# TensorE's order rewritten so that matmuls of one array mode stand together, PSUM's banks as they were

## The chip, the cores and the metric

The kernel runs on one core of a Trainium2 chip. The metric is the device time of the whole program in microseconds, the median of several runs. The five engines (TensorE or PE, VectorE or DVE, ScalarE or ACT, Pool, and SyncE which issues the DMAs) each run their own instruction list in order and meet only through semaphores.

## The reference

Eight blocks ("batches") of 512 tokens by 256 features go through one adaptive-layer-norm transformer block:

```python
h = _layernorm(x, axis=-1) * (1 + ca) + sa
x = x + ga * _L0_attn_ref(h, ...)      # 16 heads of 16 features, softmax over 512 keys
h = _layernorm(x, axis=-1) * (1 + cb) + sb
x = x + gb * _L0_ffn_ref(h, ...)       # 2 shared and 16 routed experts (top 4), gelu
```

All 18 experts are computed for all tokens: up (256 to 128 features), gelu, times the gate (zero for experts not chosen), down (128 to 256). ca, sa, ga, cb, sb, gb come from one small product per batch.

## The kernel before

**Staging.** A software pipeline runs over batches. One iteration i does attention for batch i, the projections for batch i + 1, and the experts of batches i - 1 and i - 2 (`true_item` gives each kind its lag). An iteration has four sets, s = 0 to 3; a set is one group of four heads. `slot_order(s)` (line 70) writes a set's order by hand as a list of items (kind, number); every engine walks the same list and does its part of each item it knows. So this list is TensorE's order, and VectorE's, ScalarE's and Pool's too. `NO_MAX` (line 67) and `EXTRAS` place items by slot.

**A set.** A set has U = 16 slots, then the ups, then pv:

- in a slot, `max` (one score matmul of the next head group; VectorE reduces it to a row maximum, `neg_max`, line 765) and `exp` (one transposed score matmul of this group; ScalarE takes its exponent into `probs`, line 573). Both have 64 rows of contraction. Units of even number use array rows 0 to 63, odd ones 64 to 127 (`unit`, at = 64 * (u % 2)). Moving size 512. TensorE's line is 871.
- between them 20 or 16 `down` items a set (three full-array matmuls each, line 960; accumulated in two `down_bank`s), and the extras: transposes of the attention output (`oT`, line 913), of normalised rows (`onT`, `h1T`, `h2T`, line 905), products `wo`, `qk`, `v`, `logit` (line 822), the gates' transpose `gateT` (944), VectorE's norms (`stats`, `rows`, lines 629 to 639), the router's top four (`top`, lines 690 to 701) and `final`.
- then four or five `up` items (six full-array matmuls each, line 822; ScalarE gelu, line 618, VectorE times the gate, line 755, ScalarE and Pool split into two half-precision parts, lines 563 and 529), `maxT` (the transposed maxima, line 878, copied by VectorE into the score operand, line 773, which the next set's `exp` matmuls wait for), and `pv` (four items of four 32-column matmuls in float32, line 894, into `pv_bank`, which VectorE copies to `o_raw` at the end of the set, line 812).
- the first two `exp` of the next set (EARLY = 2) stand in the pv part.

Before, a slot issues one max and one exp. A few slots have no max (`NO_MAX`), so two or three maxima of a set are left over for the ups.

**Banks.** PSUM's eight banks: two `vector_bank`s, used in turn by every item of `V_KINDS` (max, maxT, oT, wo, v, logit, gateT), three `scalar_bank`s in turn for `R_KINDS` (exp, onT, h1T, qk, h2T, up), one `pv_bank`, two `down_bank`s. `ring` gives each item its bank by its place in the order; `wait_bank` makes TensorE wait until the bank's user before has been read. No bank of either kind can be filled while its previous content is unread, and TensorE's list goes on only after the wait.

Of the kernel before, what the change touches and what calls it, by code (L numbers as in the profile page):

```python
# [57 lines left out]
EARLY = 2  # L58
# [5 lines left out]

NO_MAX = {0: (3, 5, 8), 1: (0, 11, 12), 2: (0, 10), 3: (0, 15)}


def slot_order(s):  # L70


    out = []
    maxima = [("max", (s + 1) * U + u) if s < 3 else ("max0", u) for u in range(U)]
    downs = [("down", d) for d in range(TT * SETS[DOWN_SET[s]], TT * SETS[DOWN_SET[s] + 1])]
    ups = [("up", c) for c in range(*SETS[UP_SET[s]:UP_SET[s] + 2])]
    for u in range(U):
        out += EXTRAS.get((s, u), [])
        if u not in NO_MAX[s]:
            out.append(maxima.pop(0))  # L80
        if u >= EARLY:
            out.append(("exp", s * U + u))
        left = U - 1 - u
        while downs and len(downs) * (U - 1) > left * TT * SETLEN:
            out.append(downs.pop(0))
    assert not downs
    for j, up in enumerate(ups):
        out += EXTRAS.get((s, U + j), [])
        if j == 3:
            out += maxima + [("maxT", s + 1) if s < 3 else ("maxT0", 0)]  # L90
            maxima = []
        out.append(up)
        if j < 2:
            out += maxima[:2]
            maxima = maxima[2:]
        if j >= 1:
            out.append(("gated", up[1] - 1))
        if j >= 3:
            out.append(("pv", s * TT + j - 3))
    out.append(("gated", ups[-1][1]))  # L100
    for kc in range(len(ups) - 3, TT):
        out.append(("pv", s * TT + kc))
        if kc >= TT - EARLY:
            out.append(("exp", (s + 1) * U + kc - TT + EARLY) if s < 3 else ("exp0", kc - TT + EARLY))
    return out


# [9 lines left out]
def true_item(item):  # L117

    kind, n = item
    if kind in ("max0", "maxT0", "exp0"):  # L120
        return kind[:-1], n, 1
    if kind in ("h1T", "qk", "v", "stats1", "rows1"):
        return kind, n, 1
    if kind == "up" or kind == "gated":
        return kind, n, -1 if SET_OF[n] < 2 else -2
    if kind == "down":
        return kind, n, -1 if SET_OF[n // TT] < 1 else -2
    if kind == "final":
        return kind, n, -2
    return kind, n, 0 if kind in ("max", "maxT", "exp", "pv", "xg") else -1  # L130


def ring(kinds, banks):
# [31 lines left out]
def block_kernel(nc, x, c_t, wmod, wqkvo, bqk_in, bv, bo, w_up, w_down, router, out):  # L165
# [7 lines left out]
    with ctx:  # L173
# [449 lines left out]
        def _(dve):  # L623
# [92 lines left out]
            def body(i, par):  # L716
                nb, pb = i + 1, i - 1
                x_post, z = x_post2[1 - par], z2[1 - par]
                for s in range(G):
                    for item, kind, n, b in items(i, s):  # L720
# [27 lines left out]
                        if kind == "gated" and n >= NSH:  # L748

                            g = gelu[:, n % NGELU, :]  # L750
                            wait(dve, taken["up"], NEX, b, n + 1)
                            quarter, rest = divmod(n - NSH, 4)
                            if rest == 0:
                                wait(dve, s_gld[quarter % 2], 32, b, 16 * (quarter // 2 + 1))
                            dve.tensor_tensor(g, g, gates[:, (n - NSH) % 8, :], ALU.mult).then_inc(s_gated, 1)  # L755
                        if item[0] not in V_KINDS:
                            continue
                        src = bank(item)
# [46 lines left out]
                        elif kind == "gateT":  # L805
                            wait(dve, s_gst, 16, b, 0)
                            dve.tensor_copy(gate_rows, src[0:NR, :]).then_inc(done, 1)

                    if exists(i):
                        wait(dve, made["pv"], G * TT, i, TT * (s + 1))  # L810
                        wait(dve, made["oT"], 4, i, 0)
                        dve.tensor_copy(o_raw[:, s, :], OB[:]).then_inc(taken["pv"], 1)

            iterations(dve, body)

# [179 lines left out]
```

## Time and profile before

| | |
|---|---|
| median of 3 runs | 1061.0 us (1059.8 to 1061.09) |
| the profiled execution | 1056.59 us, span 1054.8 us |
| PE busy | 942.0 us (89%), 5928 matmuls |
| DVE busy | 677.4 us (64%) |
| ACT busy | 630.0 us (60%) |
| POOL busy | 379.3 us (36%) |
| mean granted TensorE clock | 0.945 |
| maxima (line 765) | 512, mean 688 ns |
| exponents (line 573) | 512, mean 603 ns |

The profile is of one execution. Busy time of PE is modelled with overlapping matmuls, so the start of one matmul to the start of the next says more than its duration. In a timeline row the columns are start, duration, engine, line, operation, output and inputs, tile and shapes, count, and in brackets the idle time before it and who ended it. "PEclk" is the granted share of full clock.

### The profile page before, as it was taken

What the parts mean: (1) busy time and instruction counts of PE and PEld (TensorE: products, weight loads), DVE (VectorE), ACT (ScalarE), POOL (GpSimd) and SP (SyncE); (2) the same over time, 40 slices, a digit from 0 to 9 for tenths busy, and PEclk for the clock granted to TensorE, in tenths of its full rate; (3) what the DMA queues carried; (4) which work ended last, traced back from release to release, by engine and by line L of the source; (5) the groups of instructions that cost most, each with busy time, mean ns of one, the idle gap of its engine ahead of it and who ended that gap; (6) DMA issues with size and microseconds to landing.
All of it is one profiled execution on the core that took longest, in us unless ns stands there. A gap on an engine that the chain in (4) does not pass through costs nothing.

```text
span 1054.8 us, 17394 instructions
## 1 busy us (share of the span) xinstructions
PE 942.0 (89%) x5928; PEld 423.0 (40%) x5928; DVE 677.4 (64%) x1315; ACT 630.0 (60%) x1033; POOL 379.3 (36%) x325
## 2 busy tenths in 40 slices
PE   5468786889999999999999999999999999997897
PEld 3112222324444354434444354444444453345564
DVE  5665767656776777676866567676866677724333
ACT  3145644556676758666775647666675757662343
POOL 4331222232442434243433324243434332344354
PEclk9658978989999999999999989999999999999899
DMA  6811600352016210342017210352016200311220
GB/s 217 170 45 36 111 1 1 68 144 101 1 36 141 96 61 4 86 144 101 1 36 180 86 36 1 87 146 101 1 36 177 77 24 1 107 65 40 74 113 21
DMA packets 50428, 78.53 MB, mean 74 GB/s; under 512 B 8216, under 2 KB 44568, under 8 KB 46240
## 3 DMA queue, kind: packets, MB, share of 16 engines
q1 hardware_dynamic: 50336, 77.36, 26.2%
q8 instruction: 51, 0.84, 0.4%
q14 instruction: 41, 0.34, 0.1%
HBM read 64.31 MB, written 12.89 MB: 73 GB/s over the span
## 4 chain that ended last, share of the span: by engine, by line
PE 73%; DVE 9%; DMA 4%; ACT 4%; issue 4%; POOL 2%; SPq 2%; DVEq 0%; POOLq 0%; ACTq 0%
PE scalar_bank L822 20%; PE down_bank L960 19%; PE vector_bank L871 11%; PE pv_bank L894 10%; DVE neg_max L765 5%; PE scalar_bank L871 5%; PE vector_bank L822 4%; PE scalar_bank L905 2%; PE vector_bank L913 2%; ACT probs L573 1%; SPq L389 1%; DMA gates_by_expert<-rows 1%; DMA k_parts<-qk_lo 1%; POOL act_lo L529 1%; DMA gates<-gates_by_expert 1%
## 5 line engine op out<-in xcount | busy, mean ns | idle before, releaser
L765 DVE TENSOR_REDUCE neg_max<-vector_bank 128x1 f16<-128x512 f32 x512 | 339.4, 688 | 143.2 <-PE vector_bank L871 133.2
L573 ACT ACTIVATE probs<-scalar_bank 128x512 f32<-128x512 f32 x512 | 290.6, 603 | 206.4 <-PE scalar_bank L871 203.6
L529 POOL TENSOR_TENSOR act_lo<-gelu,act_hi 128x512 f16<-128x512 f32 x144 | 177.3, 1251 | 201.9 <-ACT act_hi L563 192.0
L871 PE MATMUL vector_bank<-k_aug,q_aug 64*128 64x512 f16 x512 | 194.6, 413 | 42.7 <-DVE neg_max L765 25.7
L871 PE MATMUL scalar_bank<-q_aug,k_aug 64*128 64x512 f16 x512 | 200.0, 406 | 9.7 <-ACT f_ring L546 3.3
L960 PE MATMUL down_bank<-down_hi,act_hi 128*128 128x256 f16 x576 | 163.3, 283 | 0.3
L960 PE MATMUL down_bank<-down_lo,act_hi 128*128 128x256 f16 x576 | 159.9, 278 | 0.0
L960 PE MATMUL down_bank<-down_hi,act_lo 128*128 128x256 f16 x576 | 159.6, 277 | 0.0
L755 DVE TENSOR_TENSOR gelu<-gelu,gates 128x512 f32<-128x512 f32 x128 | 110.6, 885 | 69.6 <-ACT gelu L618 59.5
L618 ACT ACTIVATE gelu<-scalar_bank 128x512 f32<-128x512 f32 x144 | 85.1, 596 | 76.4 <-PE scalar_bank L822 54.7
L894 PE MATMUL pv_bank<-probs,v_aug 128*32 128x512 f32 x1024 | 130.6, 620 | 0.0
L563 ACT ACTIVATE act_hi<-gelu 128x512 f16<-128x512 f32 x128 | 79.9, 627 | 50.2 <-DVE gelu L755 50.1
L822 PE MATMUL scalar_bank<-z_hi,up_hi 128*128 128x512 f16 x288 | 109.8, 381 | 0.0
L822 PE MATMUL scalar_bank<-z_lo,up_hi 128*128 128x512 f16 x288 | 109.2, 379 | 0.0
L822 PE MATMUL scalar_bank<-z_hi,up_lo 128*128 128x512 f16 x288 | 109.2, 379 | 0.0
L871 PEld LDWEIGHTS vector_bank<-k_aug,q_aug 64*128 64x128 f16 x512 | 43.2, 94 | 160.2 <-issue 79.8
L960 PEld LDWEIGHTS down_bank<-down_hi,act_hi 128*128 128x128 f16 x576 | 56.4, 98 | 96.3 <-issue 87.4
L477 POOL TENSOR_TENSOR z_lo<-f_ring,z_hi 128x512 f16<-128x512 f32 x32 | 37.2, 1174 | 128.4 <-ACT f_ring L602 86.7
L871 PEld LDWEIGHTS scalar_bank<-q_aug,k_aug 64*128 64x128 f16 x512 | 45.8, 94 | 87.6 <-issue 58.0
L477 POOL TENSOR_TENSOR qk_lo<-f_ring,qk_hi 128x512 f16<-128x512 f32 x32 | 37.0, 1156 | 105.1 <-ACT f_ring L594 104.6
L773 DVE COPY q_aug<-vector_bank 1x512 f16<-1x512 f16 x128 | 53.9, 421 | 11.9 <-PE vector_bank L878 10.2
L960 PEld LDWEIGHTS down_bank<-down_hi,act_lo 128*128 128x128 f16 x576 | 57.4, 100 | 7.7
(122 smaller groups left out, 1104.8 us busy)
## 6 DMA issues: line engine op xcount, KB each, us to landing
gates<-gates_by_expert SPq DMA_DIRECT2D x32, 1024.0 KB, 4.7
q_aug<-q_parts SPq DMA_DIRECT2D x48, 128.0 KB, 3.9
k_aug<-k_parts SPq DMA_DIRECT2D x48, 128.0 KB, 4.5
x_pre<-in_x SPq DMA_DIRECT2D x8, 512.0 KB, 6.0
x_post<-in_x SPq DMA_DIRECT2D x8, 512.0 KB, 3.9
out<-x_post SPq DMA_DIRECT2D x8, 512.0 KB, 5.0
gates<-in_w_up SPq DMA_DIRECT2D x4, 576.0 KB, 11.6
gates<-in_w_down SPq DMA_DIRECT2D x4, 576.0 KB, 5.5
```

The source lines that it names most:

```text
L477: pool.tensor_tensor(lo, f_ring[:, n % 2, :], hi, ALU.subtract).then_inc(s_lo, 1)
L529: pool.tensor_tensor(act[1][:, c, :], gelu[:, n % NGELU, :], act[0][:, c, :], ALU.subtract).then_inc(s_elo, 1)
L563: scalar.activation(act[0][:, c, :], gelu[:, n % NGELU, :], ACT.Copy).then_inc(s_ehi, 1)
L573: scalar.activation(probs[:, n % U, :], src[:], ACT.Exp, scale=SCALE).then_inc(taken[kind], 1)
L618: scalar.activation(gelu[:, n % NGELU, :], src[:], ACT.Gelu).then_inc(taken[kind], 1)
L755: dve.tensor_tensor(g, g, gates[:, (n - NSH) % 8, :], ALU.mult).then_inc(s_gated, 1)
L765: dve.tensor_reduce(neg_max[:, (u // 2) % TT, at:at + 1], src[:], AX.X, ALU.max, negate=True).then_inc(done, 1)
L773: ins = dve.tensor_copy(qa[at:at + 1, 2 * n + j // 2, :], src[:].bitcast(F16)[32 * j:32 * j + 1, 0:S])
L822: ins = pe.matmul(dst, a, b, start=n == 0, stop=n == len(terms) - 1)
L871: pe.matmul(dst[:], st[at:at + 64, pair, t * P:(t + 1) * P], mo[at:at + 64, pair, :], start=True, stop=True).then_inc(sig, 1)
L894: ins = pe.matmul(o, v_aug[par][:, kc, at], probs[:, u, :], start=kc == 0, stop=kc == TT - 1)
L960: ins = pe.matmul(o, act[a][:, c - SETS[SET_OF[c]], t * P:(t + 1) * P], wd[w][:, c, :], start=c == 0 and k == 0 and t % 2 == 0, stop=c == ...
```

## The change

`slot_order` is rewritten, and with it the order of all engines. Two slots become one: two maxima, then two exponents, then the downs of two slots. No slot is without a maximum, `NO_MAX` is gone, and none are left for the ups. `maxT` stands two ups after the slots, not three. The two early exponents stand before pv, together, and the four pv items follow one another. VectorE's copy of `pv_bank` to `o_raw` becomes an item of its own, `oraw`, at the end of the set. The banks' number and the rule of turns stay; which item has which bank follows from the new order.

```diff
--- before.py
+++ after.py
@@ -64,44 +64,34 @@
 
 
 
-NO_MAX = {0: (3, 5, 8), 1: (0, 11, 12), 2: (0, 10), 3: (0, 15)}
-
-
 def slot_order(s):
 
 
     out = []
     maxima = [("max", (s + 1) * U + u) if s < 3 else ("max0", u) for u in range(U)]
+    early = [("exp", (s + 1) * U + u) if s < 3 else ("exp0", u) for u in range(EARLY)]
     downs = [("down", d) for d in range(TT * SETS[DOWN_SET[s]], TT * SETS[DOWN_SET[s] + 1])]
     ups = [("up", c) for c in range(*SETS[UP_SET[s]:UP_SET[s] + 2])]
     for u in range(U):
         out += EXTRAS.get((s, u), [])
-        if u not in NO_MAX[s]:
-            out.append(maxima.pop(0))
-        if u >= EARLY:
-            out.append(("exp", s * U + u))
+        if u % 2:
+            out += maxima[u - 1:u + 1]
+            out += [("exp", s * U + v) for v in (u - 1, u) if v >= EARLY]
         left = U - 1 - u
         while downs and len(downs) * (U - 1) > left * TT * SETLEN:
             out.append(downs.pop(0))
     assert not downs
     for j, up in enumerate(ups):
         out += EXTRAS.get((s, U + j), [])
-        if j == 3:
-            out += maxima + [("maxT", s + 1) if s < 3 else ("maxT0", 0)]
-            maxima = []
+        if j == 2:
+            out.append(("maxT", s + 1) if s < 3 else ("maxT0", 0))
         out.append(up)
-        if j < 2:
-            out += maxima[:2]
-            maxima = maxima[2:]
         if j >= 1:
             out.append(("gated", up[1] - 1))
-        if j >= 3:
-            out.append(("pv", s * TT + j - 3))
+    out += early
     out.append(("gated", ups[-1][1]))
-    for kc in range(len(ups) - 3, TT):
-        out.append(("pv", s * TT + kc))
-        if kc >= TT - EARLY:
-            out.append(("exp", (s + 1) * U + kc - TT + EARLY) if s < 3 else ("exp0", kc - TT + EARLY))
+    out += [("pv", s * TT + kc) for kc in range(TT)]
+    out.append(("oraw", s))
     return out
 
 
@@ -127,7 +117,7 @@
         return kind, n, -1 if SET_OF[n // TT] < 1 else -2
     if kind == "final":
         return kind, n, -2
-    return kind, n, 0 if kind in ("max", "maxT", "exp", "pv", "xg") else -1
+    return kind, n, 0 if kind in ("max", "maxT", "exp", "pv", "oraw", "xg") else -1
 
 
 def ring(kinds, banks):
@@ -753,6 +743,11 @@
                             if rest == 0:
                                 wait(dve, s_gld[quarter % 2], 32, b, 16 * (quarter // 2 + 1))
                             dve.tensor_tensor(g, g, gates[:, (n - NSH) % 8, :], ALU.mult).then_inc(s_gated, 1)
+                        if kind == "oraw":
+
+                            wait(dve, made["pv"], G * TT, b, TT * (n + 1))
+                            wait(dve, made["oT"], 4, b, 0)
+                            dve.tensor_copy(o_raw[:, n, :], OB[:]).then_inc(taken["pv"], 1)
                         if item[0] not in V_KINDS:
                             continue
                         src = bank(item)
@@ -805,11 +800,6 @@
                         elif kind == "gateT":
                             wait(dve, s_gst, 16, b, 0)
                             dve.tensor_copy(gate_rows, src[0:NR, :]).then_inc(done, 1)
-
-                    if exists(i):
-                        wait(dve, made["pv"], G * TT, i, TT * (s + 1))
-                        wait(dve, made["oT"], 4, i, 0)
-                        dve.tensor_copy(o_raw[:, s, :], OB[:]).then_inc(taken["pv"], 1)
 
             iterations(dve, body)
```

The order of a set's TensorE items, as both functions give it, for set 3 before (cut) and after (cut):

```
before: max0 | down0 down1 | max1 exp50 | down2 | max2 exp51 | down3 | max3 exp52 | down4 down5 | ... up5 | max14 max15 | up6 up7 maxT up8 | pv12 | up9 | pv13 pv14 | exp0 | pv15 | exp1
after:  max0 max1 | down0 1 2 | max2 max3 exp50 exp51 | down3 4 5 | max4 max5 exp52 exp53 | down6 7 | ... up5 up6 maxT up7 up8 up9 | exp0 exp1 | pv12 13 14 15
```

## Rows read from the trace of the kernel before

**Rows 1.** The page's chain of work that ended last: shares of the span by engine.

```profile
PE 73%; DVE 9%; DMA 4%; ACT 4%; issue 4%; POOL 2%; SPq 2%; DVEq 0%; POOLq 0%; ACTq 0%
```

**Rows 2.** Windows, one steady iteration: stretch, length, busy time of each engine, granted clock.

```profile
479.30:595.60 116.30, 112.23 (x738) 49.90 (x737) 82.39 (x162) 79.02 (x130) 43.15 (x38) 1.00 0.27 76
```

**Rows 3.** Waits of PE over the whole run: total us, times, longest.

```profile
PE vector_bank L871 <- DVE neg_max L765: 25.7, 51, 1.9
```

**Rows 4.** Timeline of PE, a slot of set 3 with one down.

```profile
582.79 0.39 PE L871 MATMUL vector_bank<-k_aug,q_aug 64*128 64x512 f16 x1
582.79 0.39 PE L871 MATMUL scalar_bank<-q_aug,k_aug 64*128 64x512 f16 x1
583.11 0.28 PE L960 MATMUL down_bank<-down_hi,act_hi 128*128 128x256 f16 x1
...
583.34 0.27 PE L960 MATMUL down_bank<-down_hi,act_lo 128*128 128x256 f16 x1
583.54 0.39 PE L871 MATMUL vector_bank<-k_aug,q_aug 64*128 64x512 f16 x1
```

**Rows 5.** Timeline of PE, start of set 0.

```profile
486.47 0.60 PE L871 MATMUL vector_bank<-k_aug,q_aug 64*128 64x512 f16 x2
487.00 0.28 PE L960 MATMUL down_bank<-down_hi,act_hi 128*128 128x256 f16 x1
```

**Rows 6.** Timeline, two maxima in different banks, and VectorE's start on the first.

```profile
592.63 0.39 PE L871 MATMUL vector_bank<-k_aug,q_aug 64*128 64x512 f16 x2
...
592.95 0.39 PE L822 MATMUL scalar_bank<-z_hi,up_hi 128*128 128x512 f16 x1
...
593.05 0.70 DVE L765 TENSOR_REDUCE neg_max<-vector_bank 128x1 f16<-128x512 f32 x1 [2.11 <-PE vector_bank L871]
```

**Rows 7.** Timeline, wo's last matmul, its reading, and two maxima queued behind.

```profile
500.62 0.27 PE L822 MATMUL vector_bank<-wqkvo_hi,z_lo 128*128 128x256 f16 x1
...
500.93 0.69 DVE L790 TENSOR_TENSOR rows<-vector_bank,ga_all 128x512 f32<-128x512 f32 x1 [0.98 <-PE vector_bank L822]
...
501.54 1.28 DVE L765 TENSOR_REDUCE neg_max<-vector_bank 128x1 f16<-128x512 f32 x2
```

**Rows 8.** Timeline of PE: first up and last pv of the sets 0 to 3.

```profile
506.25 0.38 PE L822 MATMUL scalar_bank<-z_hi,up_hi 128*128 128x512 f16 x1
...
515.63 1.06 PE L894 MATMUL pv_bank<-probs,v_aug 128*32 128x512 f32 x8
...
536.52 0.39 PE L822 MATMUL scalar_bank<-z_hi,up_hi 128*128 128x512 f16 x1
...
545.91 1.06 PE L894 MATMUL pv_bank<-probs,v_aug 128*32 128x512 f32 x8
...
566.07 0.38 PE L822 MATMUL scalar_bank<-z_hi,up_hi 128*128 128x512 f16 x1
...
576.57 1.06 PE L894 MATMUL pv_bank<-probs,v_aug 128*32 128x512 f32 x8
...
591.24 0.38 PE L822 MATMUL scalar_bank<-z_hi,up_hi 128*128 128x512 f16 x1
```

**Rows 9.** Timeline of ACT, second reader of a transposed bank.

```profile
495.63 0.59 ACT L602 ACTIVATE f_ring<-scalar_bank 128x512 f32<-128x512 f32 x1
```

**Rows 10.** Timeline of DVE in set 1: norm's rows, router's first step, next maximum.

```profile
521.38 2.96 DVE L639 TENSOR_SCALAR rows<-x_pre,mean_var,rstd 128x256 f32<-128x256 f32 x4
...
529.87 0.40 DVE L690 MAX8 top<-logits 128x8 f32<-128x16 f32 x4
...
532.32 0.68 DVE L765 TENSOR_REDUCE neg_max<-vector_bank 128x1 f16<-128x512 f32 x1
```

**Rows 11.** Timeline of an early iteration without ups: pv and the copies of the maxima.

```profile
138.03 3.96 PE L894 MATMUL pv_bank<-probs,v_aug 128*32 128x512 f32 x24
138.14 1.72 DVE L773 COPY q_aug<-vector_bank 1x512 f16<-1x512 f16 x4 [0.77 <-PE vector_bank L878]
```

**Rows 12.** Windows, a stretch of the first iteration.

```profile
50.00:80.00 30.00, 20.33 (x72) 4.11 (x71) 20.97 (x41) 11.39 (x19) 8.32 (x5) 0.52 0.13 40
```

## The prediction

> **What bounds the kernel now.** I read the chain of work first: 73% of the span is TensorE, no other engine has more than 9% [rows 1]. Then one steady iteration by windows: TensorE is busy 112.2 of 116.3 us at full clock, VectorE 82, ScalarE 79 [rows 2]. Then the waits: TensorE stood 25.7 us in the whole run for VectorE's maxima [rows 3]. So it is TensorE's order, back to back, and what it costs is read in the timeline of PE [rows 4]: a maximum (64 rows, lower or upper half) and an exponent score (other half) start in the same hundredth, 582.79; the next full-array matmul starts 0.32 us later, at 583.11; the three "down" matmuls follow at 0.11 to 0.12 us, and after the last (583.34) the next score starts 0.20 us later. Two matmuls of one half follow at 0.21 us (two take 0.60, one 0.39) [rows 5]. So a score stream is 0.22, and each edge between array modes costs 0.10: a trip into the score mode and back is 0.22 + 2 x 0.10, about 0.41 us.
>
> The Trainium skill, "TensorEngine Tiling (Array Packing)", section "Key Properties", says that changing the tiling mode drains TensorE; by that rule, the trace agrees, with 0.10 us an edge.
>
> **What is removed on TensorE.** I counted the stretches of one mode in the order that both versions of `slot_order` give, set by set: 38, 36, 35, 38 before, 18, 18, 17, 18 after, so 76 edges fewer in an iteration: 76 x 0.10 = 7.6 us. Streams: before, a maximum and an exponent beside each other are sometimes in the same half (the maxima run ahead by slots that have none), and singles stand alone; taking neighbours of opposite halves as one stream I count 82 before and 64 after: 18 x 0.22 = 4.0 us. Two maxima in different banks do go together: 592.63, with the next matmul 0.32 later [rows 6]. So 11.6 us of 116.3 go if nothing else waits. The diff also keeps TensorE's other matmuls, all DMAs, ScalarE's and Pool's work as they are; the o_raw copy becomes an item but stays at the same place of VectorE's order, cost nothing.
>
> **What is added: the second maximum of a four.** There are two vector banks. Before, one maximum a slot is issued, and VectorE reads one bank while the other fills. Now TensorE issues max, max, exp, exp, in order. The second max needs the bank that VectorE empties last, and behind it wait both exponents, the downs, and all engines' later work. VectorE starts 0.42 us after the matmul (592.63, 593.05), takes 0.69, but queued ones follow at 0.59 (1.28 for two) [rows 6, 7]. So from a four's first max to both banks free: 0.42 + 0.59 + 0.69 + 0.06 = 1.76 us. TensorE's own work from the second max to the next four is 0.22 + 0.32 + 0.44 + 0.33 for each down beyond one: 1.3 us with two downs, 1.63 with three. When that is below 1.76 the steady period of two slots is their mean, (1.76 + 1.3)/2 = 1.53 and 1.70. Before, two slots of two or three downs took 1.52 and 1.84 (0.76 with one down, 0.33 for each more) [rows 4]. So in plain slots the gain is nearly gone. Where a vector-bank item (oT, wo, v, gateT) precedes a four, its bank is the one the second max needs, and that item has only just been made: wo's last matmul at 500.62, VectorE's reading 500.93 to 501.62 [rows 7], so the second max waits until 1.0 us after that matmul's start, less the 0.2 it takes anyway: 0.85 us each.
>
> **Walk through the four sets**, with those numbers, from the end of pv. Before, the sets took 30.2, 30.3, 30.65 and (116.3 less these) 25.15; their slot parts, to the first up, 19.8, 19.9, 19.2 and 13.7 [rows 8]: set 0 starts with the two maxima at 486.47 [rows 5], the others 1.0 after the last pv row before them, and the ups start at 506.25, 536.52, 566.07, 591.24.
> Set 3 has no extras. The fours fall at 2.1, 3.7, 5.0, 7.1, 8.7, 10.2, 12.1 us, and the ups start at 13.0 instead of 13.7.
> Set 0: oT1 and oT2 hold both banks before the first four (1.0 us of waits), oT3 0.85, exp7 finds its scalar bank held by a transpose whose second reader, 0.6 long, is not done (0.6) [rows 9], wo0 itself waits 0.8 for a maximum behind the layer-norm statistics, wo0 and wo1 then 0.85 each. Ups start at 22.4 instead of 19.8.
> Set 1: rows of the second norm come before the first maxima, as before, and the second max then waits 0.6. h2T1 now shares its bank with h2T0 and waits 0.6 for ScalarE. The norm of 2.96 us [rows 10] starts later, and h1T0 waits 1.25 for it (0.55 before); the next second max 0.6, logit 0.3. Worst is the router: VectorE is in it from 529.87 to 532.32 [rows 10]. Before, two slots without a maximum cover those 2.45 us; now a four stands there, and the next four waits 1.65 + 0.6. Ups start at 22.8 instead of 19.9.
> Set 2: maxima 50 and 51 wait 1.2 and 0.6, then 0.75 behind gateT, 0.9 behind v0, 0.3 + 0.5 at v1. Ups at 19.95 instead of 19.2.
> The rest of a set gets shorter: before, 10.4 us (four ups) and 11.5 (five) from first up to pv's end, with three score trips (set 0 and 1) or two trips and two pv edges (2 and 3); now one trip: 10.4 - 3 x 0.41 + 0.42 = 9.55, and 10.85. The early exponents stand ahead of pv and need the copies of the transposed maxima, 1.72 us [rows 11]; two or three ups of 1.3 us cover that, 0.1 is left in set 1.
> Sums after: 22.4 + 9.55 = 31.95; 22.8 + 9.6 = 32.4; 19.95 + 10.85 = 30.8; 13.0 + 10.85 = 23.85. Together 119.0 against 116.3: +2.7 us, from +1.8, +2.1, +0.15, -1.3. The 11.6 saved are met by some 14 us of new waits.
>
> **Over the run.** Sets 0 to 2 come six times with full work: 6 x 4.05 = 24.3. Set 3 five times: -6.5. Its last time there are exponents only, 16 trips become 8 and 16 streams 8: -0.2 x 8 - 0.22 x 8 = -3.4. The first two iterations have few downs and ups. There nothing covers the copies: the copies run from 138.14 for 1.72 us while pv is already under way, from 138.03 [rows 11]. Now pv waits for them behind the exponents: 1.8 us later, less the score trips inside pv of 2 x 0.41: about +1.0 each in six sets, bounded by -0.8 and +2.3. With the waits behind extras, the same two iterations give +7 in all (from 0 to 14). Sum: 24.3 - 6.5 - 3.4 + 7 = +21.4. The profiled execution has 1056.6 us (span 1054.8 and 1.8 around it), 0.4% under the median of 1061.0: 1078 on that, 1082 on the median.
>
> **Rivals.** First, TensorE's saving survives in full, because the bank waits are hidden: 11.6 us over some 6.6 iterations' worth (five whole ones, the sixth without set 3's maxima, and the first two in part) is 76, so 985 on the median. For it speaks TensorE's 73% of the chain; against it that VectorE has 11 us of maxima (16 x 0.69) in slots of 13 us, and that a wait stands in TensorE's in-order queue.
> Second, the waits are there but half as long, since VectorE's and TensorE's waits partly take each other's place: 11.6 - 7 = 4.6 us x 6.6 = 30 faster: 1031. The decisive point is whether the second max finds its bank free more often than my walk says; the break-even is 11.6 us of new waits an iteration, a fifth fewer than I count, and there it is within 0.2%.
> Third, the clock. Where TensorE was busy 20.3 of 30 us it was granted 0.52, so mostly the lower level, 1.2 GHz [rows 12]; now its busy share in an iteration falls from 0.97 to some 0.85. If the mean grant fell from 1.00 to 0.95, 100 us of matmuls take 5 more: 33 over the run, 1115.
> The skill's "TensorE: Matmul & The Clock Gate", section "A second HAM failure mode: psum-queue depth-cycling", says that micro-idles from cycling through PSUM banks can make the clock swing; in the full iterations here 4 us of idle did not do it.
> Fourth, the change doesn't do what it says: two maxima side by side would not run together. The row of two says they do [rows 6]; I give it nothing of its own.
>
> **How the numbers follow.** My forecast, 1082 (own range 1064 to 1100), 0.63; clock, 1115, 0.10; within 0.2% (about what a measurement can tell from no change), 0.05; half the waits, 1031, 0.17; full saving, 985, 0.05. Slower 0.73, same 0.05, faster 0.22. The range from 1030 to 1108 leaves out the full saving, some of the case of half the waits and most of the clock's.
>
> **What would show it.** In the profile after: TensorE's wait for neg_max grows from 25.7 us to 70 or more and its busy time falls; the second matmul of a max pair starts later than the first in most fours; behind a wo a gap of 0.85; behind the router one of about 2 us; set 3's slots 13 us, and sets 0 and 1 22 to 23. It would be wrong if fours mostly start within 0.1 us whole, if the sets with extras are shorter than before, or if the clock leaves 1.00 in the full iterations.

## The result, and the profile after

The changed kernel takes 1115.7 us where the kernel before takes 1061.05 in the same comparison: ratio 1.0499 [1.0462, 1.0535], 55 us slower. The direction was forecast; the size was not, and 1115.7 lies above the range's upper end of 1108. The profiled execution's span is 1114.3 us against 1054.8. A fourth execution of the changed kernel took 1517.7 us at a mean granted clock of 0.553, which no other execution of this case shows; it is left out of the ratio.

The page of the kernel after: busy time of each engine, the granted clock in 40 slices, the chain's shares.

```profile
PE 937.6 (84%) x5928; PEld 446.0 (40%) x5928; DVE 672.0 (60%) x1315; ACT 617.1 (55%) x1033; POOL 387.5 (35%) x325
PEclk9757877699989998999999978999989998899799
...
PE 63%; DVE 18%; issue 6%; ACT 4%; DMA 4%; POOL 2%; SPq 2%; DVEq 0%; ACTq 0%; POOLq 0%
```

TensorE does the same 5928 matmuls and is busy 4 us less, yet the span is 59.5 us longer. On the chain TensorE fell from 73% to 63% and VectorE rose to 18%, where no other engine had more than 9% [rows 1]. The mean granted clock is 0.910, before 0.945. What TensorE waited for (us in total, times, longest):

```profile
PE vector_bank L861 <- DVE neg_max L760: 40.7, 70, 2.2
PE scalar_bank L895 <- DVE rows L629: 26.2, 11, 5.8
PE scalar_bank L861 <- DVE q_aug L768: 15.6, 9, 3.1
...
PE scalar_bank L895 <- ACT f_ring L536: 9.9, 15, 2.7
...
PEld vector_bank L861 <- DVE neg_max L760: 89.8, 133, 2.7
```

The first row was 25.7 us in 51 waits [rows 3], so it grew by 15 us only; the same wait of the weight loads, the last row, was 69.5 in 117. The view does not tell the whole of the wait, as set 3 in the timeline of PE shows (start, duration, what; in brackets the idle time):

```profile
618.14 0.39 PE L861 MATMUL vector_bank<-k_aug,q_aug 64*128 64x512 f16 x1
618.74 0.39 PE L861 MATMUL vector_bank<-k_aug,q_aug 64*128 64x512 f16 x1 [0.21 <-DVE neg_max L760]
618.82 0.52 PE L861 MATMUL scalar_bank<-q_aug,k_aug 64*128 64x512 f16 x2
```

The second maximum starts 0.60 us after the first, VectorE's period of 0.59 [rows 7], and not beside it; only 0.21 of that is called idle, since the first one's modelled duration covers the rest. So the starts are read, and with them the lengths of the sets. A set is measured from the start of the last `pv` matmul of the set before to the start of its own last one, and its first part to the first `up`. All lengths of this kind below are worked out in the same way from the matmul starts in each trace.

| set, iteration | before: length, to the first up | after | forecast after |
|---|---|---|---|
| 0, it. 4 | 30.17, 19.73 | 31.45, 21.88 | 31.95, 22.4 |
| 1, it. 4 | 30.28, 19.83 | 35.90, 26.30 | 32.4, 22.8 |
| 2, it. 4 | 30.66, 19.10 | 31.38, 19.95 | 30.8, 19.95 |
| 3, it. 4 | 25.17, 13.61 | 24.08, 12.94 | 23.85, 13.0 |
| 1, its. 2, 3, 5, 6 | 30.15, 29.82, 29.82, 30.47 | 33.50, 34.47, 35.53, 35.73 | 32.4 |

Added up over the run, after less before:

| part | forecast | measured |
|---|---|---|
| set 0, six times | +10.5 | +11.8 |
| set 1, six times | +12.6 | +27.1 |
| set 2, six times | +0.9 | +5.8 |
| set 3, five times, and the last | -6.5, -3.4 | -3.9, -3.9 |
| first two iterations | +7 | +20.3 |
| tail | 0 | +2.3 |
| sum | +21.4 | +59.5 |

Two parts carry most of the miss: set 1, and the first two iterations. In set 0 iteration 5 alone has 5.3 of the 11.8 us (42.22 us after, 36.94 before). TensorE stands there twice, 3.20 and 3.43 us, for nothing that the view names, and its grant is 0.63 in the 14 us from the set's start. What it waits for there is open.

Set 1 of iteration 4 in stretches (busy time of each engine, then the granted clock, DMA share and GB/s):

```profile
549.40:552.00 2.60, 0.36 (x6) 0.06 (x2) 2.49 (x5) 1.24 (x3) 1.27 (x2) 1.00 0.00 0
552.00:559.00 7.00, 6.03 (x25) 3.04 (x26) 5.04 (x12) 4.20 (x7) 2.28 (x2) 0.52 0.00 0
559.00:568.50 9.50, 7.32 (x74) 4.18 (x72) 6.46 (x23) 6.58 (x12) 2.35 (x3) 1.00 0.01 2
568.50:573.00 4.50, 4.29 (x17) 1.93 (x17) 1.42 (x3) 1.08 (x2) 0.00 (x0) 0.62 0.00 0
573.00:585.30 12.30, 12.24 (x81) 4.67 (x79) 6.24 (x10) 10.59 (x17) 6.21 (x5) 1.00 0.33 77
```

TensorE's timeline at the start of that set and behind the router:

```profile
549.37 0.39 PE L861 MATMUL vector_bank<-k_aug,q_aug 64*128 64x512 f16 x2
552.39 1.11 PE L895 MATMUL scalar_bank<-ident,rows 128*128 128x128 f32 x4 [2.63 <-DVE rows L629]
553.44 0.76 PE L861 MATMUL vector_bank<-k_aug,q_aug 64*128 64x512 f16 x2
...
568.18 0.39 PE L861 MATMUL vector_bank<-k_aug,q_aug 64*128 64x512 f16 x1 [1.65 <-DVE neg_max L760]
568.78 0.39 PE L861 MATMUL vector_bank<-k_aug,q_aug 64*128 64x512 f16 x1 [0.21 <-DVE neg_max L760]
...
570.56 0.63 PE L812 MATMUL scalar_bank<-h_hi,wqkvo_hi 128*128 128x512 f16 x1
...
573.57 0.38 PE L812 MATMUL scalar_bank<-h_hi,wqkvo_hi 128*128 128x512 f16 x1
```

The wait behind the router is as forecast to the hundredth, 1.65 and then 0.60 from start to start; iterations 3 to 6 all have it. What was not forecast stands behind the waits: after 2.63 us of nothing the clock is granted at 0.52 for 7 us, nearly all of it the lower level, 1.2 GHz, and after the router's wait at 0.62 for 4.5 us. The router's wait does not always do it: in iteration 3 it is 1.64 us (to 447.46), and the grant stays at 1.00 behind it. The same 128x512 product is 0.63 us at the low grant and 0.38 at 2.4 GHz. And the first wait is itself longer than the 1.60 of the kernel before, for the same transposes. VectorE and Pool in front of it, then the four `rows` instructions alone (shortest, median, longest, in ns):

```profile
549.51 0.69 DVE L750 COPY o_raw<-pv_bank 128x512 f32<-128x512 f32 x1 [1.00 <-PE pv_bank L884]
550.12 2.22 DVE L629 TENSOR_SCALAR rows<-x_post,mean_var,rstd 128x256 f32<-128x256 f32 x4
...
550.71 1.15 POOL L519 TENSOR_TENSOR act_lo<-gelu,act_hi 128x512 f16<-128x512 f32 x1 [1.19 <-ACT act_hi L553]
...
L629 DVE TENSOR_SCALAR rows<-x_post,mean_var,rstd x4: 400/407/1256, 550.1 to 551.9; 128x256 f32<-128x256 f32 x4
```

And in the kernel before, the same place of the same iteration:

```profile
517.37 1.41 DVE L639 TENSOR_SCALAR rows<-x_post,mean_var,rstd 128x256 f32<-128x256 f32 x4
...
L639 DVE TENSOR_SCALAR rows<-x_post,mean_var,rstd x4: 401/402/437, 517.4 to 518.4; 128x256 f32<-128x256 f32 x4
...
518.83 0.66 PE L905 MATMUL scalar_bank<-ident,rows 128*128 128x128 f32 x4 [1.60 <-ACT probs L573]
```

The view names ScalarE's exponent as what ended the 1.60, but the transposes need the rows too, and these end at 518.78, 0.05 us ahead of them. Three rows take 0.40 us after and one takes 1.26, and Pool's `act_lo` of 1.15 lies over it: the long row starts at 550.76 and ends 0.16 us after `act_lo` does. So it is in set 1 of each of the iterations 2 to 7, where the longest row takes 1.25 to 1.27. Pool is late because the early exponents now stand ahead of the last `gated`: ScalarE does two exponents before the last `act_hi`, and Pool's half comes after that. The Trainium skill, "SBUF — State Buffer", section "Who interferes with whom", lists `tensor_scalar` among the VectorE operations that can take the port pair shared with GpSimd when their operands allow it, and calls that pair an exclusive lock, so that the loser blocks for a whole instruction. The trace agrees with a block of one row, 0.86 us over its 0.40.

The other part is in the first iterations, where no `up` stands around `maxT`. The kernel after there, timeline of PE and two windows of the same columns as above:

```profile
127.70 0.38 PE L868 MATMUL vector_bank<-ident,neg_max 128*128 128x128 f16 x4 [0.68 <-DVE neg_max L760]
129.99 0.61 PE L861 MATMUL scalar_bank<-q_aug,k_aug 64*128 64x512 f16 x2 [1.91 <-DVE q_aug L768]
130.53 6.23 PE L884 MATMUL pv_bank<-probs,v_aug 128*32 128x512 f32 x32
136.70 0.39 PE L861 MATMUL vector_bank<-k_aug,q_aug 64*128 64x512 f16 x2
...
514.35 3.64 PE L884 MATMUL pv_bank<-probs,v_aug 128*32 128x512 f32 x32
...
127.60:130.50 2.90, 0.89 (x6) 0.37 (x6) 1.68 (x4) 0.36 (x1) 0.00 (x0) 0.74 1.18 123
130.50:137.00 6.50, 6.50 (x36) 1.48 (x34) 0.16 (x1) 1.09 (x2) 3.09 (x2) 0.59 0.74 183
```

The exponents wait 1.91 us for the copies and pv waits behind them, as forecast (1.8). Then the 32 pv matmuls take 6.2 us at a clock of 0.59, where they take 3.64 at full clock (the row of 514.35, from a full iteration). From `maxT` to the next set's first maximum it is 9.0 us.

### The profile page after: what moved, and what is told of

The parts are those of the page before. It is cut to its first block, busy times and chain, and to the rows that moved or that the text cites. A ratio compares the mean times of both kernels' runs of the same rounds, so it can differ in the third digit from the quotient of the medians.

```text
span 1114.3 us, 17394 instructions
## 1 busy us (share of the span) xinstructions
PE 937.6 (84%) x5928; PEld 446.0 (40%) x5928; DVE 672.0 (60%) x1315; ACT 617.1 (55%) x1033; POOL 387.5 (35%) x325
## 4 chain that ended last, share of the span: by engine, by line
PE 63%; DVE 18%; issue 6%; ACT 4%; DMA 4%; POOL 2%; SPq 2%; DVEq 0%; ACTq 0%; POOLq 0%
PE scalar_bank L812 17%; PE down_bank L950 14%; PE pv_bank L884 11%; DVE neg_max L760 8%; PE vector_bank L861 7%; PE scalar_bank L861 4%; PE vector_bank L812 4%; PE scalar_bank L895 3%; DVE rows L629 2%; PE vector_bank L903 1%; DVE q_aug L768 1%; ACT f_ring L536 1%; DVE stats L619 1%; POOL act_lo L519 1%; SPq L379 1%
## 5 line engine op out<-in xcount | busy, mean ns | idle before, releaser
L563 ACT ACTIVATE probs<-scalar_bank 128x512 f32<-128x512 f32 x512 | 277.9, 598 | 293.8 <-PE scalar_bank L861 264.4
L760 DVE TENSOR_REDUCE neg_max<-vector_bank 128x1 f16<-128x512 f32 x512 | 326.6, 686 | 131.1 <-PE vector_bank L861 128.9
L519 POOL TENSOR_TENSOR act_lo<-gelu,act_hi 128x512 f16<-128x512 f32 x144 | 184.2, 1295 | 206.2 <-ACT act_hi L553 195.4
L861 PE MATMUL vector_bank<-k_aug,q_aug 64*128 64x512 f16 x512 | 158.3, 423 | 75.9 <-DVE neg_max L760 40.7
L745 DVE TENSOR_TENSOR gelu<-gelu,gates 128x512 f32<-128x512 f32 x128 | 117.9, 938 | 102.6 <-ACT gelu L608 88.8
L950 PE MATMUL down_bank<-down_lo,act_hi 128*128 128x256 f16 x576 | 164.0, 285 | 0.0
L861 PE MATMUL scalar_bank<-q_aug,k_aug 64*128 64x512 f16 x512 | 141.2, 417 | 19.7 <-DVE q_aug L768 15.6
L861 PEld LDWEIGHTS vector_bank<-k_aug,q_aug 64*128 64x128 f16 x512 | 36.6, 94 | 203.9 <-DVE neg_max L760 89.8
L895 PE MATMUL scalar_bank<-ident,rows 128*128 128x128 f32 x192 | 37.3, 336 | 36.4 <-DVE rows L629 26.2
L884 PEld LDWEIGHTS pv_bank<-probs,v_aug 128*32 128x32 f32 x1024 | 32.0, 118 | 76.0 <-issue 76.0
## 6 DMA issues: line engine op xcount, KB each, us to landing
gates<-in_w_up SPq DMA_DIRECT2D x4, 576.0 KB, 11.8
```

Of the source, the lines that this page charges most:

```text
L519: pool.tensor_tensor(act[1][:, c, :], gelu[:, n % NGELU, :], act[0][:, c, :], ALU.subtract).then_inc(s_elo, 1)
L563: scalar.activation(probs[:, n % U, :], src[:], ACT.Exp, scale=SCALE).then_inc(taken[kind], 1)
L760: dve.tensor_reduce(neg_max[:, (u // 2) % TT, at:at + 1], src[:], AX.X, ALU.max, negate=True).then_inc(done, 1)
L861: pe.matmul(dst[:], st[at:at + 64, pair, t * P:(t + 1) * P], mo[at:at + 64, pair, :], start=True, stop=True).then_inc(sig, 1)
L884: ins = pe.matmul(o, v_aug[par][:, kc, at], probs[:, u, :], start=kc == 0, stop=kc == TT - 1)
L895: ins = pe.transpose(dst[:, t * P:(t + 1) * P], rows[:, t, n * P:(n + 1) * P], ident[:])
```

## The experiments

All ratios are to the kernel before, with a 95% interval.

| run | edit | median us | ratio | clock of the profiled run |
|---|---|---|---|---|
| after | | 1115.7 | 1.0499 [1.0462, 1.0535] | 0.910 |
| e1_fill | after, both fills | 1086.8 | 1.0249 [1.0197, 1.0301] | 0.948 |
| e6_fill_h2 | after, first fill | 1094.4 | 1.0301 [1.0234, 1.0367] | 0.936 |
| e2_set1_old | set 1 as before | 1083.8 | 1.0222 [1.0169, 1.0275] | 0.932 |
| e3_fours_only | fours, pv part as before | 1086.8 | 1.0248 [1.0197, 1.0300] | 0.929 |
| e4_pv_only | slots as before, new pv part | 1098.2 | 1.0357 [1.0303, 1.0412] | 0.926 |
| e5_gated_first | last `gated` ahead of the early exponents | 1105.7 | 1.0412 [1.0341, 1.0482] | 0.919 |
| e7_after_short | after, maxima over 64 columns | 1047.3 | 0.9879 [0.9821, 0.9937] | 0.937 |
| e8_before_short | before, the same | 1036.0 | 0.9766 [0.9709, 0.9822] | 0.951 |
| e10_three_vector_banks | after, banks 3 + 2 | 1133.7 | 1.0665 [1.0594, 1.0735] | 0.919 |
| e11_fours_three_banks | e3, banks 3 + 2 | 1075.2 | 1.0118 [1.0061, 1.0175] | 0.935 |
| e12_fours_fill | e3 and both fills | 1064.9 | 1.0025 [0.9999, 1.0051] | 0.955 |
| e9_set3_fours | before, fours in set 3 | 1056.3 | 0.9964 [0.9931, 0.9996] | 0.941 |
| e13_set3_fours_fill | e9 and seven fill matmuls in the first place | 1053.5 | 0.9929 [0.9905, 0.9953] | 0.947 |

The variants share one `slot_order` in which two tuples say which sets have the new slots (fours) and which the new pv part (cut):

```
 FOURS, NEWPV = (0, 1, 2, 3), (0, 1, 2, 3)      # after
-        if u % 2:
+        if s in FOURS:
+            if u % 2: ...                      # as after
+        else: ...                              # as before, with NO_MAX
...
+        if j >= 3 and s not in NEWPV:
+            out.append(("pv", s * TT + j - 3)) # pv part as before
```

### Does the clock make the loss? e1_fill, e6_fill_h2

Matmuls whose product is not used are put into the two long waits: nine into `h2T0`'s bank ahead of its transposes, seven ahead of maximum 44, into the bank that exponent 28 fills next. Nothing reads them.

```
+            def fill(dst, count):
+                for _ in range(count):
+                    pe.matmul(dst[:], ident16[:], ident16[:].unsqueeze(1).broadcast_to([P, 4, P]), start=True, stop=True)
...
+                        if item == ("max", 44):
+                            wait_bank(pe, ("exp", 28), i)
+                            fill(bank(("exp", 28)), 7)
...
+                                    fill(dst, 9)
```

> The changed kernel with matmuls of no use put into two waits of set 1: 9 of 512 columns ahead of h2T0 (into the bank that h2T0 will fill) and 7 ahead of maximum 44 (into exp 28's bank); about 1.9 and 1.5 us at the high clock, less than the waits of 2.6 and 1.65 us. Nothing else changes. Theory (the excess over the walk is the clock, which falls after these waits: granted 0.53 and 0.50 in the profile after): the low stretches of set 1 go, its length falls from 33.5 to 38 us to about 32.5, the run to 1095 to 1102. Rival (the excess is waiting alone, for VectorE's rows and the router, and the clock costs nothing on the chain): 1114 to 1120, set 1 as long as before.

> The changed kernel with only the first of the two fills: 9 matmuls of no use ahead of h2T0. If both waits of set 1 bring the clock down by themselves, this keeps the first low stretch (5 to 6 us long, some 2.5 to 3 us lost each time) away and leaves the one behind the router: 1096 to 1104. If one wait is enough for all of it: 1085 to 1090, as with both.

e1 gives 1086.8, 29 us less than after and 8 below the theory's range, though TensorE has 128 matmuls more. Its clock is 0.948. Granted clock by slice, then the whole of set 1 of iteration 4, then TensorE at its start:

```profile
PEclk9757878799999999999999999999999999999899
...
543.00:575.00 32.00, 29.78 (x208) 13.66 (x206) 21.55 (x50) 23.74 (x41) 12.03 (x10) 1.00 0.12 30
...
542.83 2.12 PE L868 MATMUL scalar_bank<-ident 128*128 128x512 f16 x9
545.51 0.66 PE L928 MATMUL scalar_bank<-ident,rows 128*128 128x128 f32 x4 [0.57 <-DVE rows L654]
```

The four transposes begin 2.68 us after the fill's start, so the wait for VectorE is as long as it was; but they take 0.66 and not 1.11, and the clock stays at 1.00. Set 1 has 31.2 to 31.9 us in iterations 2 to 6, 21.75 to 22.45 to the ups. Of the 32.5 us between the two spans 18.1 are in set 1 and 7.1 in set 0, nearly all of these in iteration 5 (35.22 us at a grant of 1.00, where after has 42.22). So the clock is about half of the loss (29 of 55), and without it the kernel is 26.7 us slower, where the walk forecast 21.4. e6, with the first fill alone, gives 21 of the 29, between its two expectations; set 1 still loses clock there (0.90 to 0.95 in iterations 3 to 6). The intervals of e1 and e6 overlap, so what the second fill adds is likely and not shown by the times.

### Which half of the change: e2, e3, e4

e2 gives set 1 its old slots and pv part.

> The changed kernel with set 1 alone in the order of before (slots, ups, pv); sets 0, 2, 3 new. Theory (set 1's fours stand behind VectorE's long steps and carry half of the loss): set 1 back to 30.2 us, 30 us less over six iterations and some 8 in the first two: 1075 to 1085. Rival (the walk's own +2.1 us a set is all that is in it, the rest is elsewhere and moves to another set): 1100 to 1106.

It came at 1083.8, in the theory's range, but set 1 takes 31.6 to 32.7 us in iterations 2 to 6, not the 30.2 it had: set 0's new pv part still stands ahead of it, its rows still take 2.2 us and TensorE waits 2.4 to 2.5 us for them.

e3 keeps the fours in all sets and puts back the pv part, e4 the reverse.

> The slots as in the changed kernel (fours, no slot without a maximum), the rest of each set as before (maxT ahead of the fourth up, pv between, early exponents inside pv). The walk gives the new pv part -2 us an iteration where ups cover the copies and +1 a set where they don't, so without it: 1112 to 1128. If the pv part is what costs: below 1100.

> The slots as before, with slots that have no maximum; only the pv part of the changed kernel (both early exponents ahead of pv, pv items together). The walk: one score trip fewer in sets 0 and 1 and also two pv edges fewer in 2 and 3: -0.4, -0.4, -0.6, -0.6, -13 over the run; +1 in each of six early sets: 1052 to 1060. If the exponents ahead of pv cost more (VectorE's copies of 1.72 us, ScalarE's order): 1065 to 1080.

Both went against the expectation, e3 by 25 us below it and e4 by 38 above. The fours alone cost 2.5%, the new pv part alone 3.6%, and together 5.0%. In e4 `maxT` stays ahead of the fourth `up`. Outside set 1 a full set of e3 has nearly the same length as after: set 0 31.46 and 31.45, set 2 31.10 and 31.38, set 3 24.07 and 24.08 in iteration 4 (the first number is e3's). So the new pv part gives nothing, and what I booked to it (three score trips less) is had by the fours, which leave no maxima over for the ups. With the old slots it costs: in e4 the rest of set 0 is 11.4 us and not 10.45, as its `maxT` has a single `up` behind it and the early exponents wait for the copies. That row of e4's waits has 24.0 us where after has 15.6:

```profile
PE scalar_bank L886 <- DVE q_aug L793: 24.0, 19, 1.9
```

Of the 33.8 us between the spans of after and e3, 10.4 are in set 1, where e3 has the old pv part ahead: its rows take 1.4 to 1.7 us there, not 2.2, TensorE waits 1.6 to 1.9 us for them, not 2.6 or 2.7, and the set takes 31.6 to 35.5 us in iterations 2 to 6 at a grant of 0.86 to 0.95, where after takes 33.5 to 35.9 at 0.86 to 0.90. So the new pv part costs in full iterations too, by way of VectorE's rows and the clock. e4 says the same: 17 of its 42 us over before are in set 1, and 18 in the first two iterations.

The largest part, 17.2 us, is in the first two iterations. e3 at the place that was shown of after, timeline of PE and window:

```profile
123.62 0.38 PE L893 MATMUL vector_bank<-ident,neg_max 128*128 128x128 f16 x4 [0.68 <-DVE neg_max L785]
124.02 2.78 PE L909 MATMUL pv_bank<-probs,v_aug 128*32 128x512 f32 x24
126.74 0.39 PE L886 MATMUL scalar_bank<-q_aug,k_aug 64*128 64x512 f16 x1
127.05 1.06 PE L909 MATMUL pv_bank<-probs,v_aug 128*32 128x512 f32 x8
128.05 0.39 PE L886 MATMUL scalar_bank<-q_aug,k_aug 64*128 64x512 f16 x1
128.27 0.39 PE L886 MATMUL vector_bank<-k_aug,q_aug 64*128 64x512 f16 x2
...
123.60:128.90 5.30, 5.02 (x40) 1.50 (x40) 2.40 (x6) 1.30 (x3) 0.31 (x1) 1.00 1.14 167
```

pv covers the copies, the clock stays at 1.00, and from `maxT` to the next maximum it is 4.65 us instead of 9.0: 4.35 us for one reordering, of which 1.91 is the wait and the rest the slow pv behind it. The seven sets from set 1 of iteration 0 on take 173.9 us before, 190.1 after, 175.1 in e3, and with set 0 of iteration 0 the first two iterations end at 255.5, 275.8 and 258.5. So of the +20.3 in the table above all but 3 us are the new pv part's.

### The rows: e5_gated_first

```
     if s in NEWPV:
+        out.append(("gated", ups[-1][1]))
         out += early
-        out.append(("gated", ups[-1][1]))
```

> The changed kernel with the last gated item of each set put ahead of the two early exponents instead of behind them; TensorE's order is unchanged. In the changed kernel ScalarE holds the last act_hi behind the exponents (which wait for pv), so Pool's act_lo, 1.15 us, falls on VectorE's norm rows at the start of set 1, which take 2.21 us instead of 1.41. Theory (Pool's overlap makes the rows longer, the longer wait sends the clock down): rows at 1.4 to 1.5 us, TensorE's wait before h2T0 from 2.6 to 1.8 us, and the low stretch behind it gone or rarer: set 1 at 33 to 34.5 us, the run 1095 to 1106. Rival (the overlap is a coincidence): rows stay at 2.2, 1112 to 1118.

1105.7 against 1115.7, with intervals that just overlap, so that the gain is likely and not shown by the times. The rows at the start of set 1 take 1.62 to 1.95 us, no more 2.2, and not the 1.4 to 1.5 expected, and TensorE waits 2.1 to 2.4 us for them and not 1.8; the longest row of iteration 4 (same columns as above):

```profile
L654 DVE TENSOR_SCALAR rows<-x_post,mean_var,rstd x4: 401/402/974, 546.8 to 548.3; 128x256 f32<-128x256 f32 x4
```

With Pool earlier, VectorE loses less, 0.57 and not 0.86. Again the long row ends 0.14 us after the `act_lo` that lies over it, and the wait shrinks with the rows. The direction is as the theory of the shared port has it, but it is a small share, since set 1 still has 31.7 to 35.7 us and the run's mean clock is 0.919: the wait for the rows remains long enough for the clock to fall in some iterations.

### The price of a maximum: e7, e8

Both reduce 64 of 512 columns, which takes the same instruction from 0.69 to 0.22 us; the rest of the work is unchanged.

```
-                                              src[:], AX.X, ALU.max, negate=True).then_inc(done, 1)
+                                              src[:, 0:64], AX.X, ALU.max, negate=True).then_inc(done, 1)
```

> The changed kernel with VectorE's maximum over the first 64 of the 512 columns only (so the maximum that is subtracted before the exponent is not the row's): its 0.69 us fall to some 0.15. Theory (two vector banks that VectorE empties one behind the other hold TensorE's fours): the plain fours of set 3 lose their waits, its ups start at 11.3 to 11.9 us instead of 12.9; set 0 keeps the waits behind oT and wo and comes to 20 us; the run 25 to 45 us under the changed kernel and level with or under the shortened kernel before, 1020 to 1050. Rival (the loss is elsewhere, the banks cost little): set 3 at 12.7 or more, the run not under 1095.

> The kernel before with the same short maximum (first 64 columns). TensorE's order of before hardly waits for VectorE in set 3 (13.2 to 13.6 us to the first up), so it stays at 12.8 to 13.2; a few us go in sets 0 and 1: 1035 to 1056.

The kernel after gains 68 us by it, the kernel before 24. So 44 us of the loss go with the length of a maximum: its turns in two banks, and the clock behind the waits, which the two runs do not part. With short maxima the fours' saving is seen: set 3's slots take 11.3 us (after 12.9), while before (e8) has 12.8 to 14.2, of which the upper end was not expected. But in sets 0 and 1 the fours are still behind: 20.95 to the ups in set 0 against 19.05, 22.7 to 23.8 in set 1 against 18.8 to 21.8. These two have the most items other than maxima in the vector banks (oT, wo, logit), and their readers are as slow as before; that this is the reason is argued and not measured. Even so, after is 11 us slower than before, and not level as the theory had it. Between the two spans the first two iterations give +10.8 us, set 1 +14.4 (at a grant of 0.88 to 0.95) and set 3 -16.7.

### A third bank: e10, e11

```
-NV, NRB = 2, 3
+NV, NRB = 3, 2
```

> The changed kernel with three vector banks and two scalar banks instead of two and three, nothing else. Theory (the second maximum and what follows oT, wo, v wait for a bank): the waits for maxima fall, set 3's ups start at 11.5 to 12.0 us, set 0's at 19.5 to 20.5; the scalar side may give back 1 us in set 1 with its transposes; the run 1070 to 1095. Rival (two scalar banks hold the exponents and ups as much): 1105 to 1130.

> Fours in the slots, the pv part as before, three vector and two scalar banks. If the two causes add (banks, and exponents ahead of pv), 25 to 30 us under the run with three banks and the new pv part: 1045 to 1065. If the scalar banks bind: 1085 or more.

The waits of the maxima shrink where a third bank should take them: set 3 to the ups 12.4 (12.9; expected 11.5 to 12.0), set 0 19.3 to 19.6 (21.9; iteration 5 apart). But the run takes 1133.7 us, above even the rival's range. The bank has to come from the scalar side, and e10's waits show where the loss moved, with a place from its timeline:

```profile
PE scalar_bank L886 <- ACT gelu L633: 36.7, 28, 5.9
PE vector_bank L886 <- DVE neg_max L785: 21.1, 31, 1.8
...
426.31 0.39 PE L886 MATMUL scalar_bank<-q_aug,k_aug 64*128 64x512 f16 x1 [1.37 <-ACT gelu L633]
```

The exponents wait for ups whose gelu is not done, the early ones ahead of pv above all. Set 1 grows to 36 or 37 us, set 2 to 33 to 36. With the old pv part (e11) it is 1.2% over before, against 2.5% with 2 + 3 banks. At 1075.2 us it lies between its two expectations, and 58 us under e10, not 25 to 30: with two scalar banks the new pv part costs more. Its sets 0 are 28.9 to 30.2 us (iteration 5 apart), below the 30.0 to 30.55 of before, while set 1 is 35 to 36. So the walk's cause for set 0 stands, the second maximum's bank, and this PSUM has no bank to spare for it.

### Putting back what helps: e9, e12, e13

e9 has the fours in set 3 alone, where no extras stand between the slots (`FOURS, NEWPV = (3,), ()`). e12 is e3 with the fills, e13 is e9 with seven fill matmuls ahead of `h2T0`.

> The kernel before with fours in set 3's slots alone (the set without extras); its pv part and sets 0 to 2 as before. Theory (fours pay where nothing else stands in the vector banks and TensorE never waits long): set 3 goes from 24.8 to 24.1 us in five iterations, from 23.6 to some 20 in the last with exponents, and 2 to 4 us less in the second: 1049 to 1056. Rival (any fours bring waits that send the clock down or delay set 0): 1060 or more.

> Fours in the slots, the pv part as before, two vector banks, and both fills of e1 in set 1. If the clock's share is apart from the pv part's, 15 to 20 us under the 1087 of the fours without fills: 1066 to 1072. If the old pv part had already kept the clock up: 1083 to 1088.

> Fours in set 3 only (e9) and 7 matmuls of no use ahead of h2T0 in set 1, where this order waits 1.6 to 1.8 us. Theory (the set of before sits at the edge: after some of these waits the clock falls too, and the fill keeps it): set 1 at 30.2 in every iteration instead of 30.3 to 31.3, the second iteration 3 us shorter: 1048 to 1054, clear of the kernel before. Rival (only the longer waits of the changed kernel bring the clock down): 1055 to 1060, as without fill.

e9 is faster than before by 0.4% [0.04, 0.7]: set 3 takes 24.06 to 24.4 us instead of 24.75 to 25.2, the last one 21.07 instead of 23.61, 5.8 us in all, while set 1 gives back 4.2 in iterations 2 to 6, where its grant is 0.945 in four of five. e12, with the fours in all sets and the waits filled, is 22 us under e3 and where before is, 1.0025 [0.9999, 1.0051]: with the clock held, the waits of the fours take back about what the edges give. e13 is the fastest of the runs with whole maxima, 1053.5 us or 0.71% [0.47, 0.95] below before. What the fill does is seen in the granted clock of set 1 of iteration 2, first e9, then e13:

```profile
285.00:316.00 31.00, 28.92 (x200) 12.71 (x192) 22.28 (x49) 24.00 (x39) 11.72 (x11) 0.94 0.13 31
```

```profile
285.00:316.00 31.00, 28.96 (x199) 13.01 (x199) 22.66 (x50) 23.95 (x40) 11.69 (x11) 1.00 0.14 31
```

e9 waits 1.77 us at the start of this set and is granted 0.84 and 0.82 in the two stretches of 5 us behind it; the kernel before waits 1.75 there and keeps 1.00. The fill keeps it too; set 1 of iteration 1 is 25.13 us with it and 26.88 without, in iterations 2 to 6 it is 30.3 to 30.8 and not 30.3 to 31.3, and the 30.2 throughout that was expected is not reached. The intervals of e9 and e13 overlap, so that the fill adds to e9 is likely and not shown by the times.

## Why the prediction was right or wrong

**The saving on TensorE was there.** With short maxima, a whole set 3 takes 22.5 us in the new order (e7) and 24.4 or more in the old (e8): at least 1.9 us less, where the count has 20 edges fewer, 2.0 us. And e12 breaks even although its maxima wait. The other sets do not show it apart.

**The walk was close where only banks decide.** To the first up, in iterations 2 to 6, with the forecast in brackets: set 0 21.8 to 22.4 (22.4; iteration 5 apart, which has 32.1 where before has 26.4), set 2 19.95 to 19.96 (19.95), set 3 12.93 (13.0), and set 1 21.75 to 22.45 in e1 (22.8), where the clock is held. The rest of set 0 is 9.57 (9.55; the terms as written give 9.59). The rest of set 2 is 11.15 to 12.0 and of set 3 11.1 (10.85); with slots of 13.2 us in most of before's sets 3, and not the 13.7 that I walked from [rows 8], this makes most of the 7.5 us by which these two are over the forecast. That e1, with the clock held, is 26.7 us over before, near the sum's 21.4, is in part luck: by the spans the first two iterations have +17.5 of it (forecast +7), and all the rest +9.5 (forecast +14.4).

**The step that failed is the clock, a term that the sum put at nothing.** The text dismissed it with 4 us of idle in an iteration that "did not do it". Those 4 us are six gaps, the longest 1.60 us; in the changed kernel the grant falls behind single gaps of 2.6 us and more, and behind the router's 1.65 us in iterations 4 to 6. The walk itself had the router's gap, 1.65 + 0.6, and knew the one at the set's start, and priced them at their length. In the runs a gap of 2.63 us is followed by 7 us at 0.52, and filling the two took back 29 us. So set 1 ran at 0.86 to 0.90 in iterations 2 to 6, and the prediction's own sign of being wrong, a clock that leaves 1.00 in the full iterations, came true. The rival had 0.10 of the chance. It priced the clock at 33 us and came to 1115; that this is so near the 29 us and the 1115.7 measured is in part luck, since its mean grant of 0.95 was assumed and its cause was the busy share, not single waits.

**The rows of set 1 were not "as before".** The early exponents, costed only for the copies, also put ScalarE's last `act_hi` and Pool's `act_lo` onto VectorE's norm. The rows went from 1.41 to 2.22 us, which is 0.8 of the 1.03 us by which the wait grew, from 1.60 to 2.63. The step that failed here is "rows of the second norm come before the first maxima, as before": the move was not followed through the other engines' queues. e5 undoes a part of it, by 10 us in the medians, and e3, with the old pv part, more.

**The pv part was mis-sized twice.** In full sets it was booked as shorter by score trips; it gives nothing there, and costs set 1 its rows and its clock (e3 against after). In the first two iterations it was put at +7 with its waits behind extras, bounded at 14, and measured +20.3. The wait of 1.8 was right (1.91 measured), the pv matmuls behind it at 0.59 of the clock, 6.2 us and not 3.6, were not in the sum, although the rows of an early stretch showed a clock of 0.52 [rows 12].

**The other rivals.** Nothing of the full saving (985) is seen. Half the waits (1031): set 0 takes 31.2 to 32.5 us against the walk's 31.95 in iterations 2, 3, 4 and 6, so its waits are near the walk and not half of it. Of the other signs two held: a second maximum behind a `wo` starts 0.86 us after the first (533.05 and 533.91), and the slots of set 3 take 12.9 us. Set 1's slots, put at 22 to 23, take 24.0 to 26.3. Two maxima do run together where both banks are free (549.37, x2). The sign that I had named, 70 us of waits for neg_max, was a bad one: it is 40.7, since the view counts only what exceeds the first matmul's modelled duration.

## What to carry to other kernels

Grouping matmuls of one array mode saves its 0.10 us an edge only if each group finds its PSUM banks free; with two banks read by one engine in 0.6 us turns, a group of two waits for the second, and everything behind it in TensorE's list waits as well. A wait of TensorE has to be priced with the clock behind it (here waits of 1.6 to 1.75 us left the grant of set 1 at 1.00 in four iterations of the kernel before, and 2.63 us brought 7 us at 0.52), and where it can't be removed, matmuls of no use in it are cheap. An item moved ahead on one engine is moved on all that walk the same list: look at what each of them is then late with.

## What was not expected of the hardware

- A gap of 2.63 us on TensorE is followed by 7 us at a granted clock of 0.52; one of 1.65 us with a single matmul and 0.21 us behind it by 4.5 us at 0.62. With the gaps filled (e1) the grant of set 1 is 1.00 from iteration 2 on. What exactly decides it is open: the router's wait of 1.64 us in iteration 3 leaves the grant at 1.00, and behind a wait of 1.77 us in e9 the grant is 0.84, behind one of 1.75 us at the same place in the kernel before it is 1.00.
- Matmuls whose output nobody reads gave back 29 of 1116 us (e1), and 22 of 1087 in the order with the old pv part (e12 against e3), with no cost that the times show.
- A VectorE `tensor_scalar` of 128x256 takes 0.40 us, and 1.26 us when a Pool `tensor_tensor` of 1.15 us starts just ahead of it; where Pool's started earlier (e5), it takes 0.66 to 0.98.
- Two maxima that must take turns in their banks start 0.60 us apart, and the view of waits calls 0.21 of it idle.
